# Due times of attention's own pieces, one step earlier in a planned order of instructions

## The reference, cut to what matters

```python
q = heads(einsum(x, q_weight) * q_dc);  k = heads(...);  v = heads(...)
attn = softmax(einsum('bhqd,bhkd->bhqk', q, k) * scale)
out = einsum('bhqk,bhkd->bhqd', attn, v) @ w_weight.T * w_dc
x = x + out + (v @ u_weight.T) * u_dc
```

## Time and profile before

| what | value |
|---|---|
| median of 3 runs | 6607.86 us |
| the profiled execution: its time, its span | 6600.43 us, 6598.6 us |
| TensorE matmul busy | 6050.3 us (92%) |
| VectorE busy | 4564.2 us (69%) |
| GpSimd busy | 3207.4 us (49%) |
| ScalarE busy | 2347.9 us (36%) |
| the first half of the span (attention) | steps run from 147.7 to about 3330 us |

### The profile page before, as it was taken

The page is one execution under the profiler, slowest core; times in us unless marked ns, Lnnn a source line. Parts: engine busy times, 40 slices in busy tenths (PEclk is TensorE's granted clock), DMA queues, the critical chain, the costliest instruction groups (busy, mean ns, idle before and its releaser), DMA issues. The chain is left out here.

```text
span 6598.6 us, 73169 instructions
## 1 busy us (share of the span) xinstructions
PE 6050.3 (92%) x24000; PEld 2755.6 (42%) x24000; DVE 4564.2 (69%) x5830; ACT 2347.9 (36%) x4460; POOL 3207.4 (49%) x2625
## 2 busy tenths in 40 slices
PE   7999999999999999999986779998999989899997
PEld 3444444444444444444343324444443434444343
DVE  4655656556555555565546988889898888889882
ACT  2444434435344343444453323233232323233110
POOL 1775766667567675675742323324142333414212
PEclk8999999999999999999988899999999999999998
DMA  2222222232232322313223344434344443434433
GB/s 88 79 83 85 89 62 89 75 96 81 68 92 63 103 74 74 92 57 92 75 67 102 82 109 112 120 89 136 83 124 108 111 124 98 126 87 124 110 90 99
DMA packets 411564, 613.29 MB, mean 93 GB/s; under 512 B 58768, under 2 KB 189968, under 8 KB 410672
## 3 DMA queue, kind: packets, MB, share of 16 engines
q1 hardware_dynamic: 374320, 558.24, 30.4%
q10 hardware_dynamic: 36864, 50.38, 3.0%
HBM read 305.31 MB, written 201.38 MB: 77 GB/s over the span
## 5 line engine op out<-in xcount | busy, mean ns | idle before, releaser
L1125 POOL TENSOR_TENSOR acc<-acc,prob 128x512 f32<-128x512 f32 x1536 | 1908.3, 1279 | 963.3 <-PE bank L815 741.5
L1055 DVE TENSOR_REDUCE mx<-bank 128x1 f32<-128x512 f32 x2048 | 1314.9, 684 | 589.3 <-PE bank L785 584.5
L2064 DVE SCALAR_TENSOR_TENSOR g<-xps,bd,g 128x1024 f32<-128x1024 f32 x1024 | 1312.9, 1282 | 244.3 <-PE xps L1794 168.4
L948 ACT ACTIVATE prob<-misc 128x512 f32<-128x512 f32 x1496 | 842.9, 597 | 853.8 <-PE misc L802 690.5
L1794 PE MATMUL xps<-sx,spread 128*128 128x512 f32 x2048 | 891.8, 522 | 244.4 <-DVE g L2064 230.3
L785 PE MATMUL bank<-khat,qhat 96*128 96x512 f32 x2048 | 990.1, 534 | 39.2 <-DVE mx L1055 20.3
L2070 DVE TENSOR_SCALAR g<-g,lim 128x1024 f32<-128x1024 f32 x1024 | 872.7, 852 | 31.1
L802 PE MATMUL misc<-qhat,khat 98*128 98x512 f32 x1679 | 723.8, 461 | 59.2 <-ACT prob L948 42.8
L1794 PEld LDWEIGHTS xps<-sx,spread 128*128 128x128 f32 x2048 | 355.4, 195 | 775.9 <-DVE g L2064 463.8
L1808 PE MATMUL yps<-g,cexp 128*32 128x512 f32 x4096 | 612.6, 636 | 0.1
L785 PEld LDWEIGHTS bank<-khat,qhat 96*128 96x128 f32 x2048 | 391.2, 196 | 433.2 <-issue 299.9
(11 more groups left out here) (211 smaller groups left out, 6845.7 us busy)
## 6 DMA issues: line engine op xcount, KB each, us to landing
sx<-scratch_xhl SPq DMA_DIRECT2D x512, 128.0 KB, 5.0
scratch_dx<-dx SPq DMA_DIRECT2D x64, 512.0 KB, 2.7
scratch_xhl<-xhi SPq DMA_DIRECT2D x64, 512.0 KB, 4.0
scratch_xhl<-xn SPq DMA_DIRECT2D x64, 512.0 KB, 4.8
scratch_y<-ysb SPq DMA_DIRECT2D x512, 64.0 KB
dx_t<-scratch_dx SPq DMA_DIRECT2D x59, 512.0 KB, 6.3
y_t<-scratch_y SPq DMA_DIRECT2D x59, 512.0 KB, 3.7
xt_n<-in_x SPq DMA_DIRECT2D x112, 256.0 KB, 2.9
```

Source lines behind the costliest of these rows:

```text
L948: act.activation(to, bank[m][:, 0:QC], ACT.Exp, scale=SCALE).then_inc(sem[f"act_m{m}"], 1)
L1055: dve.tensor_reduce(self.mx2[:, h * TT + qt, c:c + 1], bank[m][:, 0:QC], AX.X, ALU.max).then_inc(sem[f"dve_m{m}"], 1)
L1125: pool.tensor_tensor(self.acc[:, a, h, :], self.acc[:, a, h, :], self.prob[:, (n % 2) * GH + h, :], ALU.add).then_inc(sem["pool_acc"], 1)
L2064: dve.scalar_tensor_tensor(self.g[:, t % 4, :], self.xps[t % 2][:, :], self.bd[:, i % 2, tl:tl + 1], self.g[:, (t - 1) % 4, :], ALU.mult, ...
```

## The change

`attend` stamps each of its pieces with a due time. The change takes 1.0 off it, for S, E, C, A, N, R, I and D alike. Costs, dependencies, banks, gates and the due times of side pieces stay as they are. The instructions are the same, in the same number; only their order within each engine's stream can differ, and the bank that a piece gets.

```diff
@@ -368,7 +368,7 @@
 
         def put(t, *a, **k):
             put_(*a, **k)
-            out[-1]["due"] = u * n_steps + t
+            out[-1]["due"] = u * n_steps + t - 1.0
         for n in range(n_steps + 3):
             if n < n_steps:
                 c, kt = divmod(n, TT)
```

## The result

The changed kernel takes 6538.31 us (median of four runs, 6535.64 to 6542.66); the kernel before, in four runs, 6604.98 us (6589.37 to 6611.81). The ratio is 0.9903, with the 95% interval [0.9884, 0.9922]: by that ratio faster by 64 us, where 31.5 us were predicted. The profiled execution took 6536.14 us, its span is 6534.3 us (before 6598.6).

A forecast was written before the change was run, and what follows sets the result against it. Matmuls bound three of four attention units, GpSimd the third of each sequence; 4.1 us in seven of these plus 2.8 in unit 30, 0 elsewhere, took 31.5 off 6607.9: 6576 us; own range 6552 to 6592, widened to 6537 to 6636.

The forecast's parts named there:

- it is in the plan in another place, not gone: Matmul-bound units: the 3.41 us VectorE statistics operation, making TensorE wait 1.77 us for a bank, only moves in the plan.
- I take 0 for each unit: The 24 attention units outside the third ones: no gain, bounds -1 to +2 us each, -24 to +48 in all.
- The third units: Third unit of each sequence, GpSimd-bound: 4.1 us shorter in each of seven, 28.7 in all, and 2.8 in unit 30.
- Start of the chain: Start of a third unit: GpSimd's first add comes 2.0 us earlier, bounds 0 and 6.3 us.
- GpSimd's own order: Third units: the last of eight normalising multiplications goes behind the last add, out of the bounding stretch, gaining 1.28 us.
- Fewer waits for E: Third units: exponentials ahead of DMA issues on ScalarE shrink GpSimd's 1.8 us of waits by 0.8, bounds 0 and 1.8.
- The cover of the eighth multiplication: After a third unit's last add: other work hides the late multiplication, cost nothing; up to 3 us if not hidden.
- What the prediction named as signs: Profile after: third units 3 to 6 us shorter, about 89; first add some 2 us earlier; other units within 2 us.
- The first (E held by DMA issues, nothing measurable): Third units: exponential still held, only the multiplication's 1.3 us in seven units remains, 9 us: 6599 us; chance 0.18.
- The second (maxima late): Unit starts: row maxima arrive late, deciding from a 4.2 us delay; 6630 us; chance 0.13, plus 0.09 for bank waits.
- The third (ScalarE not in the way): Third units: exponentials less held by DMA issues, first add 3.9 us earlier instead of 2.0; 6561 us; chance 0.10.
- The state space layer: The layer outside attention: keeps its plan and only starts earlier by what attention gains.

The follow-up runs named there:

- stat_idle: Kernel before, only the statistics' VectorE instruction L1005 placed after the chunk's last add, where GpSimd is idle: 6559.27 against 6600.71 us, ratio 0.9939.
- short_adds: Kernel before, order untouched, the four GpSimd adds of step 6 in each sequence's second unit cut to one column: 6566.39 against 6605.46 us, 0.9940.
- first_only: Kernel before with the change in all steps of each sequence's first unit and no other: 6593.24 against 6602.00 us, 0.9984.
- after_again: The changed kernel itself, run and traced a second time: 6543.84 us, 0.9905 of the kernel before.
- third_all: Kernel before with the change in all sixteen steps of each sequence's third unit and no other: 6613.34 against 6602.00 us, 1.0018.
- pool_only: Kernel before with the one-step offset for GpSimd's pieces alone, matmuls and exponentials keeping their due times: 6593.36 against 6602.00 us, 0.9987.
- three steps: Due times taken 3.0 steps early in all units in place of the change's 1.0: 6658.20 against 6599.94 us for the kernel before, 1.0089.
- two: Due times taken 2.0 steps early in place of the change's 1.0: 6521.57 against 6602.00 us for the kernel before, 0.9890; repeated, 6522.09 us, 0.9864.
- stat_in_run: Changed kernel with the statistics' VectorE instruction L1005 placed inside an uninterrupted run of GpSimd's adds: 6594.78 us in one run.

## Why the prediction was right or wrong

**The sign was right, the size was not, and most of the gain came from elsewhere.** The forecast of 6576 had its own range of 6552 to 6592; the time, 6538.31, lies below that, and only the widening for unknown costs (down to 6537) holds it. That own range doesn't follow from the stated bounds either: its upper end leaves 16 us for the 24 units, where the bound worked out for them is +48.

**The step that failed first: "it is in the plan in another place, not gone".** I had the row of the 3.41 us and took its duration for a property of the instruction. It was the length of a wait inside the instruction: 3.40 us in this run of A, 0.16 us in stat_idle, and 0.20 in short_adds, where the order is the same and only the run is broken. The row's 1.77 us of TensorE's wait was not the whole cost either: the slower matmuls behind it cost about as much as the waits. The term "I take 0 for each unit" is therefore wrong for the second units by 37 us (my bound was 1 us for each unit). What was there to be read: a 128x8 instruction that takes five times as long as a 128x512 reduction (0.69 us) and ends within 0.02 us of the end of GpSimd's run.

**The same term for the first units was also wrong, by 17 us.** The rule that matmuls bound those units hid waits for exponentials and a lower pace: in unit 8 TensorE's busy time fell from 103.43 to 101.77 us for the same matmuls, and the unit from 105.6 to 103.0. My bound of -1 us for each was too near. first_only shows 16.5 us in those units, the two executions of the changed kernel 17.3 and 19.0; which of the waits carry them isn't separated.

**The third units: 28.7 us predicted for seven, 0.1 measured in one execution, 7.5 in the other** (unit 30: 2.8 predicted, 0.7 and -2.5 measured). Term by term, from the traces of both kernels:

```
unit   length before, after   first A after start   L1108, L1114 in the stretch   gaps in it, us
  2       93.4   92.2           13.6   11.8            8, 6     7, 7                1.4   2.5
  6       93.1   89.8           13.6   11.9            8, 6     7, 7                1.1   0.1
 10       92.7   91.3           13.7   11.8            8, 6     7, 7                0.8   1.7
 14       92.6   92.0           13.6   12.5            8, 6     7, 7                0.7   1.7
 18       94.3   94.3           13.6   11.9            8, 6     7, 7                2.4   4.5
 22       93.7   98.2           13.6   11.9            8, 6     7, 7                1.7   8.1
 26       92.8   94.7           13.6   11.9            8, 6     7, 7                1.0   4.7
```

The stretch is from the first A to the last; a gap is what lies between two starts of GpSimd beyond 1.4 us. The 79 us of such a stretch hold 62 instructions of some 1.25 us. Groups of GpSimd in unit 2 of the changed kernel, from 349.7 to 429 us, beside the earlier trace rows, and GpSimd's waits beside the earlier trace rows:

```profile
L1125 POOL TENSOR_TENSOR acc<-acc,prob 128x512 f32<-128x512 f32 x48 | 59.8, 1280 | 8.3 <-ACT prob L948 5.7 <-PE bank L815 2.6
L1108 POOL TENSOR_TENSOR xt_n<-xt_n,brow 128x512 f32<-128x512 f32 x8 | 10.3, 1288 | 0.0
L1114 POOL TENSOR_TENSOR wwu<-wwu,brow 128x512 f32<-128x512 f32 x7 | 9.0, 1289 | 0.0
```
```profile
POOL wwu L1114 <- DMA wwu<-in_wwT: 9.9, 1, 9.9
POOL acc L1125 <- ACT prob L948: 5.7, 1, 5.7
POOL acc L1125 <- PE bank L815: 2.6, 1, 2.6
```

- Start of the chain: 2.0 us predicted, 1.7 measured (mean of the seven, 13.6 to 11.95). Right, and so is what is late next, E behind ScalarE's six issues. This timeline of unit 2's start answers the earlier trace rows:

```profile
344.34 4.00 ACTq L547 DMA_DIRECT2D qhat<-halves  x6
...
346.76 1.06 PE L815 MATMUL bank<-acc,V 128*32 128x512 f32 x8
...
349.05 1.07 ACT L948 ACTIVATE prob<-bank 128x512 f32<-128x512 f32 x2
...
349.71 1.27 POOL L1125 TENSOR_TENSOR acc<-acc,prob 128x512 f32<-128x512 f32 x1 [5.67 <-ACT prob L948]
```

C is done at 347.8, and the first A waits for an exponential until 349.71. As foretold, the wait for C has given way to one for E.
- GpSimd's own order: 1.3 us predicted. The eighth multiplication did go behind the last A (the timeline of the unit's end answers the earlier trace rows):

```profile
426.54 2.51 POOL L1125 TENSOR_TENSOR acc<-acc,prob 128x512 f32<-128x512 f32 x2
428.99 1.28 POOL L1108 TENSOR_TENSOR xt_n<-xt_n,brow 128x512 f32<-128x512 f32 x1
```

But one weight scaling came in: two had stood ahead of the first A, and with A earlier only one fits. I moved one kind of side work and forgot the other. Net 0.
- Fewer waits for E: 0.8 us predicted. Gaps in the stretch grew from 1.3 to 3.3 us on average, from 0.1 in unit 6 to 8.1 in unit 22, where the unit got 4.5 longer. In unit 2 it is 2.62 us for C of the second chunk, which isn't in the earlier trace rows. The largest ones don't belong to the program. In unit 22 GpSimd waits 3.4 us for the DMA of xt_n, the next sequence's input; in after_again, the same program, it doesn't wait for that DMA in unit 22, which has gaps of 2.9 us and lasts 92.7, and the seven units have gaps of 1.2 to 3.0, 2.3 on average. So some 1.0 us of the growth comes back in both executions, and the rest is scatter.
- The cover of the eighth multiplication: "I cost it at nothing. If that cover is gone it costs up to 3 us". Both were true. In the change the cover holds (fourth units -2.5 us in all); in third_all and pool_only it is gone and costs 3.3 and 2.9 us in each of seven.

So 1.7 + 0 - 2.0 is about nothing, and in the second execution 1.6 + 0 - 1.0 is 0.6 (units 1.1 us shorter on average), where I had 2.0 + 1.3 + 0.8. The step that failed here is GpSimd's stretch: I had it 2.1 us shorter, and it got no shorter.

**What the prediction named as signs.** S do come in blocks of four, the first A 1.7 us earlier, one L1108 behind the last A, and unit 6 lasts 89.8 us where it said about 89; but unit 6 is the best of the seven, and "the other units stay within 2 us" is false for the second ones.

**The rivals.** The first (E held by DMA issues, nothing measurable) is what the third units did, but not the kernel. The second (maxima late) did not occur at one step, as its count of 2 us against a slack of 4.2 said: in unit 2 of the change no S waits for them; it decides at three steps. The third (ScalarE not in the way) is what two steps bring: 7.3 us in a third unit, twice its 3.9. The Trainium skill's sentence that the prediction weighed ("DMA: Bandwidth & Descriptors", "Issuing engines are not separate DMA queues") does not fit here either: 4.00 us for six are 0.67 us each, a third of the 2.1 us from the issue of such a DMA to its landing, and in third_all TensorE waited 2.11 us for an exponential that stood behind six of them.

**The state space layer.** I took it as unchanged. Its part of the span is 10.6 us shorter in the profiled execution, with the same order. In the traces of the fifteen other runs, whose edits reach attention alone too, this part gains between -7 and 19 us on the kernel before without a relation to the edit (after_again, the very same program as the change: 7). So the 10.6 us lie within the scatter of single executions, and the gain that is explained is that of attention: 52.7 us of the 64, and 59.2 in the second execution.

## What to carry to other kernels

An instruction that takes far longer than its size says may have a wait inside it: lay its end against the ends of the other engines before taking its duration as a cost. Here the small VectorE instruction was safe where GpSimd is idle, or where GpSimd's run had a break before it; inside a run it took anything from 0.17 to 3.4 us. Trace the same program twice before explaining a difference of a few us between units. When a piece is taken out of a bounding stretch by precedence, count what takes its place, every kind of side work, and read the borders between units that have the new order and units that don't.

## What the hardware showed that I had not expected

- A VectorE instruction of 128x8 waited through several of GpSimd's back-to-back instructions: 3.40 us (TENSOR_SCALAR, from the third last A of a run to the run's end, past two ends of A) and 7.97 us (SCALAR_TENSOR_TENSOR, past six ends of A to the run's end). Where GpSimd is idle TENSOR_SCALAR takes 0.16 us.
- But a run doesn't always hold it. TENSOR_SCALAR got in after one A in stat_in_run (1.29 us) and at once in five of seven cases in two (0.17 us), and SCALAR_TENSOR_TENSOR got in at the next end of an A in all other traces (0.36 to 1.24 us), each time with the run going on behind it. At which boundary it gets in isn't settled; the end of the run always let it in.
- In the same runs VectorE's reductions from PSUM (0.69 us) and a reciprocal of 128x8 (0.18 us) were not held.
- The wait came back enlarged: 3.24 us more on VectorE cost the unit 5.2. Over seven units 17.3 us of it were TensorE's idle time and 19.1 us slower matmuls, and in the six us behind the gap its granted clock was 0.72.
